# Last layer's attention: two heads' probabilities turned together, values stationary by pairs, output made turned

## The reference, cut to what matters

```python
def attention(x, kv_d_w, q_d_w, k_u_w, v_u_w, q_u_w, rope_k_w, rope_q_w, o_w):
    ...
    scores = jnp.einsum('bqhd,bkhd->bhqk', q, k) * scale
    causal = jnp.tril(jnp.ones((s, s), dtype=bool))
    scores = jnp.where(causal[None, None], scores, jnp.finfo(scores.dtype).min)
    probs = jax.nn.softmax(scores, axis=-1)
    out = jnp.einsum('bhqk,bkhd->bqhd', probs, v).reshape(b, s, H)
    return out @ o_w
...
h = x + attention(rmsnorm(x, ln1_w), kv_d_w, q_d_w, k_u_w, v_u_w, q_u_w, rope_k_w, rope_q_w, o_w)
out = h + moe(rmsnorm(h, ln2_w), sh_gate, sh_up, sh_down, r_gate, r_up, r_down, router_w, router_b)
```

## Time and profile before

| | us |
|---|---|
| median of three runs | 3743.81 (3738.99 to 3747.11) |
| profiled execution | 3749.25 |
| its span, first to last instruction | 3747.5 |
| PE busy | 3031.9 (81%) |
| DVE busy | 2278.8 (61%) |
| ACT busy | 1506.0 (40%) |
| POOL busy | 535.2 (14%) |

### The profile page before, as it was taken

How to read it: one execution, slowest core, us unless ns; L and a number is a source line. 1 busy time by engine, 2 the same in 40 slices (tenths; PEclk the granted TensorE clock), 3 DMA queues, 4 the chain that set the end, 5 groups by cost and what they waited for, 6 DMA issues and landing times. The chain is left out here.

```text
span 3747.5 us, 63586 instructions
## 1 busy us (share of the span) xinstructions
PE 3031.9 (81%) x23988; PEld 2108.2 (56%) x24036; DVE 2278.8 (61%) x4830; ACT 1506.0 (40%) x3074; POOL 535.2 (14%) x791
## 2 busy tenths in 40 slices
PE   7677789988776888857996868789898978787878
PEld 3333368867664556534664435355555556676767
DVE  6888844442558888865655732367777754444453
ACT  4777721111346455443442112155545532223332
POOL 3101000000002222111110022222212111111000
PEclk8766689988887776768998979899999988898787
DMA  4877740000010000010002040000000021000000
GB/s 125 164 159 164 160 135 0 0 22 0 14 56 2 2 2 2 2 69 9 6 12 69 0 135 22 3 4 3 3 6 3 3 87 51 1 0 0 1 1 12
DMA packets 316495, 141.38 MB, mean 38 GB/s; under 512 B 296221, under 2 KB 305953, under 8 KB 312613
## 3 DMA queue, kind: packets, MB, share of 16 engines
q1 hardware_dynamic: 308072, 138.45, 13.7%
q10 hardware_dynamic: 8256, 0.52, 0.2%
HBM read 67.65 MB, written 3.15 MB: 19 GB/s over the span
## 5 line engine op out<-in xcount | busy, mean ns | idle before, releaser
L1238 ACT ACTIVATE l0x_pb<-l0x_ex,l0x_neg_max,l0x_q_scale 128x2048 uint16<-128x2048 f32 x128 | 267.8, 2093 | 108.2 <-POOL l0x_neg_max L1319 106.5
L1139 PE MATMUL l0x_s_ps<-l0x_kT,l0x_qT 128*128 128x512 bf16 x466 | 206.5, 539 | 111.3 <-DVE l0x_ex L1416 51.8
L1413 DVE TENSOR_SCALAR_CACHE_REDUCE l0x_ex<-l0x_s_ps 128x1024 f32<-128x1024 f32 x128 | 156.4, 1222 | 46.1 <-PE l0x_s_ps L1139 35.0
L1416 DVE TENSOR_SCALAR_CACHE_REDUCE l0x_ex<-l0x_s_ps,l0x_first_max 128x1024 f32<-128x1024 f32 x128 | 164.3, 1284 | 16.7 <-DVE l0x_ex L1413 0.5
L1139 PEld LDWEIGHTS l0x_s_ps<-l0x_kT,l0x_qT 128*128 128x128 bf16 x512 | 39.2, 111 | 204.8 <-DVE l0x_ex L1416 140.5
L263 PE MATMUL l3x_bank<-l3x_w_kv_x,l3x_ctxT 128*128 128x512 f32 x256 | 120.1, 613 | 26.6 <-ACT l3x_ctx_k L762 15.8
L1147 PEld LDWEIGHTS l0x_o_ps<-l0x_v,l0x_vT 128*128 128x128 f16 x2048 | 78.6, 104 | 59.1 <-issue 41.8
L2198 PEld LDWEIGHTS l1a_bank<-l1a_u,l1a_gm 64*64 64x64 f32 x2048 | 95.5, 194 | 15.6 <-issue 14.8
L2190 PE MATMUL l1a_bank<-l1a_r,l1a_r 32*64 32x64 f32 x2048 | 75.9, 287 | 35.0 <-DVE l1a_r L2532 33.6
L263 PE MATMUL l2f_bank<-l2f_w,l2f_ln_yT 128*128 128x352 f32 x256 | 103.5, 539 | 0.0
L2198 PE MATMUL l1a_bank<-l1a_u,l1a_gm 64*64 64x8 f32 x2048 | 98.4, 235 | 4.7 <-DVE l1a_gm L2551 4.7
(11 more groups left out here) (747 smaller groups left out, 7838.0 us busy)
## 6 DMA issues: line engine op xcount, KB each, us to landing
l2f_wproj_raw<-in_L_xattn_wproj SPq DMA_DIRECT2D x2, 2048.0 KB, 12.3
l3a_w<-in_L_attn_W SPq DMA_DIRECT2D x4, 1024.0 KB, 11.3
l2f_w<-in_L_ffn_w SPq DMA_DIRECT2D x1, 2816.0 KB, 11.6
l0x_ex<-in_ctxT SPq DMA_DIRECT2D x8, 256.0 KB, 5.0
l0a_wq<-in_L_attn_W_Q SPq DMA_DIRECT2D x1, 2048.0 KB
l0a_wk<-in_L_attn_W_K SPq DMA_DIRECT2D x1, 2048.0 KB
l0x_vT<-l0x_pb SPq DMA_TRANSPOSE x128, 3.6
l0a_wv<-in_L_attn_W_V SPq DMA_DIRECT2D x1, 2048.0 KB, 7.8
```

Source lines behind the costliest of these rows:

```text
L1139: ins = mm(s_ps[:, j * 512:(j + 1) * 512], qT[:, h, :], kT[:, h // 2, j * 512:(j + 1) * 512], start=True, stop=True)
L1238: s.activation(pb[:, h % 4, :], ex[:, h % 4, :], ACT.Exp, scale=q_scale[:, h:h + 1], bias=nb[:, h:h + 1], accum_out=sums[:, h:h + 1]).then ...
L1413: v.tensor_scalar(ex[:, h % 4, 0:1024], s_ps[:, 0:1024], 1.0, None, ALU.mult, ALU.max, accum_out=first_max[:, h:h + 1]).then_inc(o.up(scor ...
L1416: v.tensor_scalar(ex[:, h % 4, 1024:2048], s_ps[:, 1024:2048], 1.0, first_max[:, h:h + 1], ALU.mult, ALU.max, accum_out=mx[:, h:h + 1]).th ...
```

## The change

In softmax `e` now stays as it is (queries in partitions, heads by keys along them), and no diagonal blocks are built. One transpose takes two neighbouring heads: 2 x 64 keys become the 128 partitions, the queries of both sequences the columns. The values lie to match: for each sequence and each pair of heads `vv` is 128 x 32, the even head's keys and its 16 elements in the upper left, the odd head's in the lower right, zeros elsewhere. It is stationary now, and 64 columns of `pt` (the queries of one sequence) move. Four pairs write to the four groups of 32 partitions of `first`, so the output comes out turned, element by query. The sums come from a product of their own with `same_head`, 128 x 32 with two blocks of ones, stationary, and 128 moving columns: every sum stands 16 times, once for each element of the head. DVE takes the reciprocal of these 128 x 256 values and multiplies into `outT`. The values product is cut into four, so that even heads land in the upper and odd heads in the lower 64 partitions. Gone are `pb`, `out`, the second round of turning, the turning of the output and its copy; each engine's program has two rounds fewer.

```diff
-    HV = HD + 1
+    PAIRS, TWO = H // 2, 2 * HD
...
+        same_head = L.sb("same_head", [P, TWO])
+        rows_of = tuple(slice(n * S, (n + 1) * S) for n in range(2))
...
-            qT, vv = L.sb("qT", [P, H, P]), L.sb("v", [P, H, HV])
+            qT, vv = L.sb("qT", [P, H, P]), L.sb("v", [P, 2, PAIRS, TWO])
             pt = qT
-            e, pb = L.sb("e", [P, H, S]), L.sb("pb", [P, H, P])
-            mx, inv = L.sb("mx", [P, H]), L.sb("inv", [P, H])
-            out, outT, h = L.sb("out", [P, H, HD]), L.sb("outT", [P, DC, P]), L.sb("h", [P, D])
+            e = L.sb("e", [P, H, S])
+            mx, inv = L.sb("mx", [P, H]), L.sb("inv", [P, D])
+            outT, h = L.sb("outT", [P, DC, P]), L.sb("h", [P, D])
...
                 def turn(n):
                     for i in range(4):
-                        ins = nc.tensor.transpose(bank[n % 2][:, i * P:(i + 1) * P], pb[:, 4 * n + i, :], env.ident[:])
+                        u = 8 * n + 2 * i
+                        ins = nc.tensor.transpose(bank[n][:, i * P:(i + 1) * P], e[:, u:u + 2, :].rearrange("p u k -> p (u k)"), env.ident[:])
                     ins.then_inc(pT_ps.sem, 1)
...
                 pe.wait_ge(qk_ready.sem, qk_ready.value(t, 1))
-                mm(first[:, 0:D], lat[:], v_lat[:], start=True, stop=True).then_inc(heads_ps.sem, 1)
+                pe.sem_inc(order["pe"], 1)
+                for b in range(2):
+                    for n, r in enumerate(rows_of):
+                        own_heads = v_lat[:].rearrange("p (i n d) -> p n i d", n=2, d=HD)[:, n, :, :]
+                        ins = mm(first[r, b * P:(b + 1) * P], lat[:, b * S:(b + 1) * S], own_heads, start=True, stop=True)
+                ins.then_inc(heads_ps.sem, 1)
                 yield
                 pe.wait_ge(qk_ready.sem, qk_ready.value(t))
-                pe.wait_ge(lat_v_ready.sem, lat_v_ready.value(t, 2))
+                pe.wait_ge(lat_v_ready.sem, lat_v_ready.value(t))
...
                 pe.wait_ge(exped.sem, exped.value(t))
-                for n in (0, 1):
+                for n in range(2):
                     turn(n)
                 yield
-                for n in (2, 3):
-                    pe.wait_ge(pT_ready.sem, pT_ready.value(t, n - 1))
-                    turn(n)
-                yield
-                for n in (3, 4):
-                    pe.wait_ge(pT_ready.sem, pT_ready.value(t, n))
-                for i in range(H):
-                    ins = mm(first[:, i * HV:(i + 1) * HV], pt[:, i, :], vv[:, i, :], start=True, stop=True)
-                ins.then_inc(out_ps.sem, 1)
-                yield
-                pe.wait_ge(out_ready.sem, out_ready.value(t))
+                pe.wait_ge(pT_ready.sem, pT_ready.value(t))
+                pe.sem_inc(order["pe"], 1)
                 for c in range(DC):
-                    ins = nc.tensor.transpose(other[:, c * P:(c + 1) * P], out[:, 8 * c:8 * c + 8, :].rearrange("p h d -> p (h d)"), env.ident[:])
+                    for b in range(2):
+                        for i in range(4):
+                            mm(first[32 * i:32 * i + 32, c * P + b * S:c * P + (b + 1) * S], vv[:, b, 4 * c + i, :], pt[:, 4 * c + i, b * S:(b + 1) * S], start=True, stop=True)
+                    for i in range(4):
+                        ins = mm(first[32 * i:32 * i + 32, D + c * P:D + (c + 1) * P], same_head[:], pt[:, 4 * c + i, :], start=True, stop=True)
                 ins.then_inc(out_ps.sem, 1)
...
-                    s.activation(flat(pt[:, 4 * n:4 * n + 4, :]), bank[n % 2][:], ACT.Copy).then_inc(o.up(pT_ready), 1)
+                    s.activation(flat(pt[:, 4 * n:4 * n + 4, :]), bank[n][:], ACT.Copy).then_inc(o.up(pT_ready), 1)
...
-                s.activation(vv[:, :, 0:HD], first[:, 0:D].rearrange("p (h d) -> p h d", d=HD), ACT.Copy).then_inc(o.up(lat_v_ready), 1)
+                for n, r in enumerate(rows_of):
+                    s.activation(vv[r, :, :, n * HD:(n + 1) * HD], first[r, 0:D].rearrange("p (b i d) -> p b i d", b=2, d=HD), ACT.Copy).then_inc(o.up(lat_v_ready), 1)
                 yield from steps(2)
                 act.wait_ge(shifted.sem, shifted.value(t))
-                for b in range(2):
-                    r = slice(b * S, (b + 1) * S)
-                    s.activation(pb[r, :, r], e[r], ACT.Exp).then_inc(o.up(exped if b else None), 1)
+                s.activation(flat(e[:]), flat(e[:]), ACT.Exp).then_inc(o.up(exped), 1)
                 yield
                 take_turned(0)
                 take_turned(1)
-                yield
-                take_turned(2)
-                take_turned(3)
                 yield from steps(2)
-                act.wait_ge(out_ps.sem, out_ps.value(t, TURNED))
-                s.activation(flat(outT[:]), other[:, 0:D], ACT.Copy).then_inc(o.up(outT_ready), 1)
-                yield
...
-                yield from steps(10)
+                yield from steps(8)
...
-                yield from steps(4)
+                yield from steps(3)
                 dve.wait_ge(out_ps.sem, out_ps.value(t, MIXED))
-                both = first[:, 0:H * HV].rearrange("p (h d) -> p h d", d=HV)
-                v.reciprocal(inv[:], both[:, :, HD]).then_inc(o.up(), 1)
+                v.reciprocal(inv[:], first[:, D:2 * D]).then_inc(o.up(), 1)
                 dve.wait_ge(o.sem, o.at())
-                v.tensor_tensor(out[:], both[:, :, 0:HD], inv[:].unsqueeze(2).broadcast_to([P, H, HD]), ALU.mult).then_inc(o.up(out_ready), 1)
-                yield from steps(2)
+                v.tensor_tensor(flat(outT[:]), first[:, 0:D], inv[:], ALU.mult).then_inc(o.up(outT_ready), 1)
+                yield
...
+            pe.wait_ge(block_set.sem, block_set.value())
...
             for tile in tiles:
-                nc.scalar.activation(tile["blocks"][:], env.ident[:].unsqueeze(1).broadcast_to([P, H, P]), ACT.Copy, scale=0.0).then_inc(cleared.sem, 1)
+                nc.scalar.activation(tile["values"][:].rearrange("p b i d -> p (b i d)"), env.ident[:].unsqueeze(1).broadcast_to([P, 4, P]), ACT.Copy, scale=0.0).then_inc(cleared.sem, 1)
...
+            nc.gpsimd.memset(same_head[:], 0.0).then_inc(block_set.sem, 1)
+            pool.wait_ge(block_set.sem, 1)
+            for n, r in enumerate(rows_of):
+                nc.gpsimd.memset(same_head[r, n * HD:(n + 1) * HD], 1.0).then_inc(block_set.sem, 1)
+            pool.wait_ge(block_set.sem, block_set.value())
...
-                v.memset(tile["ones"], 1.0).then_inc(set_up.sem, 1)
                 v.memset(tile["shared_weight"], 1.0 / 8.0).then_inc(set_up.sem, 1)
```

More of the change, by code:

```diff
@@ L4260, in one_of_four @@
             LATENT, QK, VALUES = 1, 2, 3
-            MIXED, TURNED, PROJECTED = 1, 2, 3
-            heads_ps, lat_v_ready, qk_ready = L.sig("heads_ps", 3), L.sig("lat_v_ready", 2), L.sig("qk_ready", 2)
-            scores_ps, shifted, exped, pT_ps, pT_ready = L.sig("scores_ps"), L.sig("shifted"), L.sig("exped"), L.sig("pT_ps", 4), L.sig("pT_ready", 4)
-            out_ps, out_ready, outT_ready, logits_ps, scored = L.sig("out_ps", 3), L.sig("out_ready"), L.sig("outT_ready"), L.sig("logits_ps"), L.sig("scored")
+            MIXED, PROJECTED = 1, 2
+            heads_ps, lat_v_ready, qk_ready = L.sig("heads_ps", 3), L.sig("lat_v_ready", 3), L.sig("qk_ready", 2)
+            scores_ps, shifted, exped, pT_ps, pT_ready = L.sig("scores_ps"), L.sig("shifted"), L.sig("exped"), L.sig("pT_ps", 2), L.sig("pT_ready", 2)
+            out_ps, outT_ready, logits_ps, scored = L.sig("out_ps", 2), L.sig("outT_ready"), L.sig("logits_ps"), L.sig("scored")
             hid_ps, silu, hid_ready, hidT_ps, hidT_ready = (L.sig(x, NE) for x in ("hid_ps", "silu", "hid_ready", "hidT_ps", "hidT_ready"))
@@ L4486, in one_of_four @@
             return {"tensor": tensor_program, "scalar": scalar_program, "gpsimd": gpsimd_program, "vector": vector_program,
-                    "blocks": pb, "ones": vv[:, :, HD:HV], "shared_weight": cw[:, 0:1]}
+                    "values": vv, "shared_weight": cw[:, 0:1]}
         tiles = [one_of_four(n, bank[2 * n:2 * n + 2]) for n in range(WAYS)]
-        set_up, cleared = L.sig("set_up", 2 * WAYS), L.sig("cleared", WAYS)
+        set_up, cleared = L.sig("set_up", WAYS), L.sig("cleared", WAYS)
+        block_set = L.sig("same_head_set", 3)
         block = L.block()
```

## The result

| | before | after |
|---|---|---|
| median, us (lowest to highest, runs) | 3742.96 (3738.99 to 3747.11, 4) | 3699.54 (3692.00 to 3704.11, 4) |
| ratio to before (95% interval) | | 0.9881 (0.9867 to 0.9895) |
| profiled execution, us | 3749.25 | 3692.00 |
| last layer, first statistics of the norm to the last sum, us | 313.27 | 270.28 |
| last exponential to the first `h`, pass 1 / pass 2, us | 34.99 / 34.95 | 13.10 / 13.41 |

What follows compares the result with a forecast made beforehand. PE was busiest, mixing slow through its 128-column weight loads; after the change DVE's division binds. 20.7 us a pass, 2 x 20.7 = 41.4 us off the 3743.81 us median gives 3702.4 us, range 3697 to 3708.

Steps and rivals of the forecast that it cites:

- Exponential and turning: Before mixing: one exponential for two, gaining 1.07 us on tile 3; PE turns from 3483.10 for 1.97 us.
- Mixing: Tile 0's products on PE: 1.89 us at 1.2 GHz plus 0.2 drain; 1.41 us a tile at 2.4 GHz.
- nothing here goes faster than 29: In mixing on PE: no matmul takes under 29 ns, giving 1.41 us a tile at 2.4 GHz.
- Division: DVE's reciprocal of 256 elements 1.77 us, with product and gaps 2.27 us a tile, 9.1 for four; sets the pace.
- Output: After division: PE projects tiles 0 to 2 as outputs come; DVE starts L4465 right after the last division, 3496.27.
- After it: Around L241: PE idles 5 us before, 13 us at the lower clock carried over; 0, with 1.5 us either way.
- Start and values product: Layer start and tile 3's values product: memsets hidden; values between 0.2 us gained and 0.2 lost; both taken as 0.
- pairs only: Rival in mixing, chance 0.18: four column groups overlap no more than two; 3714.4 us, or 3706.0 if the clock rises.
- one after another: Rival in mixing, chance 0.05: no overlap of column groups; 6.8 or 3.4 us a tile, 3739.4 or 3712.0 us.
- The cheap reciprocal: Rival in division, chance 0.06: DVE needs only 0.92 us a tile, mixing binds; 23.3 us a pass, 3697.2 us.
- the drain at each change of group: Rival in mixing, chance 0.03: each change of column group drains PE, 0.33 us each, 9.8 us a tile; 3763.2 us.

Runs made afterwards that it cites:

- the run with the copy: Changed kernel with a plain copy of the 128 x 256 sums in place of their reciprocal: median 3691.02 us, ratio 0.9867.
- the two orders: Changed kernel with mixing products ordered one column group after another, or two groups by turns: 3703.26 us (ratio 0.989) and 3698.04 us in one run.
- The run with straight output: Changed kernel with probabilities stationary (64 columns), 34 columns moving, output turned and copied afterwards: median 3703.18 us, ratio 0.9883.
- its padded form: Straight-output kernel with the moving side padded with zeros from 34 to 64 columns: median 3698.44 us, ratio 0.9873; in a later comparison 3694.78 us.

## Why the prediction held, step by step

The forecast was 3702.4 us, the median is 3699.54. It summed to 20.7 us a pass, measured were 21.9 and 21.5. The mechanism held: narrow weights make mixing short, and then the reciprocal sets the pace. Two terms were off in size, both to the dear side; in pass 1 mixing of tile 0 gave 0.5 us more than forecast, the divisions 0.6, and what is ahead of mixing 0.1. The forecast stands within 3 us of the median, less than the 12 us by which the runs of one kernel scatter, so such closeness is partly luck.

- Exponential and turning. PE was to turn 1.11 us after the exponential starts, for 1.97 us; it was 1.10, and 1.90 to the start of mixing. The sixteen banks of the earlier trace rows became eight, and mixing never waits for ACT's copies.
- Mixing, the first mis-sized term. The prediction gave 1.89 us to tile 0 and 0.2 to the drain; the first reciprocal came 1.60 us after mixing started in pass 1 and 1.90 in pass 2. At 1.2 GHz the rates were nearly right: in the rows below 16 matmuls with 64 moving columns take 0.43 us (27 ns each, 29 forecast) and the 8 with 128 take 0.43 us (54 each, 60 forecast). What the sum missed is that the clock rises within tile 0, which it had left at 1.2 GHz. Together 0.2 to 0.5 us a pass. At 2.4 GHz the step "nothing here goes faster than 29" failed: there the 64-column ones are 14 ns apart (0.22 us for 16, 3473.59 to 3473.81 above), and a tile takes 0.88 us, not 1.41. 29 ns in the earlier trace rows is what two halves by turns give, and was taken for a floor of the engine. This error cost the forecast nothing, only because the division hides the tiles behind the first.

```profile
3470.47 0.65 PE L4324 MATMUL l3f_bank<-l3f_qT,l3f_v 128*32 128x64 f32 x16
3470.90 0.65 PE L4326 MATMUL l3f_bank<-l3f_qT,l3f_same_head 128*32 128x128 f32 x8
3471.33 0.45 PE L4324 MATMUL l3f_bank<-l3f_qT,l3f_v 128*32 128x64 f32 x16
```

- Division, the second. The reciprocal was sized at 1.77 us from the earlier trace rows; all eight lie between 1.747 and 1.758 us:

```profile
L4455 DVE RECIPROCAL l3f_inv<-l3f_bank x8: 1747/1748/1758, 3472.1 to 3614.7; 128x256 f32<-128x256 f32 x8
```

The tile came to 2.12 us and not 2.27, for the product and the next reciprocal overlap:

```profile
3473.86 0.42 DVE L4457 TENSOR_TENSOR l3f_outT<-l3f_bank,l3f_inv 128x256 f32<-128x256 f32 x1
3474.21 1.75 DVE L4455 RECIPROCAL l3f_inv<-l3f_bank 128x256 f32<-128x256 f32 x1
```

The product starts at 3473.86 with 0.42 us, and the reciprocal starts 0.35 us later. The prediction had added a gap of 0.04 us to each; the one behind the reciprocal is there, the one behind the product isn't. Four tiles are 8.50 us in place of 9.1. That DVE sets the pace was the central claim, and the run with the copy confirms it.
- Output. The projection of tile 0 was to be done by the end of the last division; `h` starts at 3480.57, 0.34 us after the last product starts (3480.23), with no wait. Right.
- After it. PE idled 5.36 us before L241 (5 predicted) and L241 took its 1.97 us at the lower level. The granted clock rose at about 3498.7, 11.5 us after L241, where 13 had been carried over from the earlier trace rows; DVE's routing is the bound in that stretch, so the difference doesn't show. Worth 0, right: `h` to the first last sum is 64.53 us against 64.46, 64.28 against 64.27 in the second pass.

```profile
3487.20 1.97 PE L241 MATMUL l3f_bank<-ident,l3f_rms_y 128*128 128x128 f32 x8 [5.36 <-DVE l3f_rms_y L224]
```

- Start and values product. Up to the last exponential pass 1 has 0.29 us less than before, a little more than the 0.2 us of gain that was allowed: from the first values product of tile 3 to the first score it is 0.87 us in place of 1.15. POOL's memsets (0.12 and 0.27 us) aren't waited for.

Of the rivals, "pairs only" and "one after another" fell in the trace of the changed kernel and by the two orders; both had been priced too high (1.18 and 2.33 us a tile at 2.4 GHz, where 1.89 and 3.4 stood). The cheap reciprocal fell by 1.75 us, and the drain at each change of group by the 18.4 ns from one matmul to the next, with no "issue" but 0.33 us ahead of the first load. The chance given to "pairs only", 0.18, was a chance for 1.89 to 3.7 us a tile against 1.41 to 1.89; the orders measured 1.18 against 0.88.

What the prediction didn't see is how little of the gain hangs on the stationary values. It credited mixing's fall from 22.80 us to narrow weights, and rightly; but these don't need the values to be stationary. The run with straight output has 64-column weights and 128 matmuls, as many as before, and takes 7.05 us at 1.2 GHz for it, and its padded form 4.44 with the clock rising on the way. Pairing and 64-column weights carry the gain, and the turned output trades a turn and a copy for 1.5 us more of reciprocal a tile.

## What to carry to other kernels

Weights in disjoint groups of columns, issued by turns, overlap: the order of the loop decides (48.6, 24.6 and 18.4 ns a matmul for one, two and four groups), so put the group innermost. Before a denominator is replicated by a block of ones so that the output comes out turned, price the reciprocal by its elements a partition (0.26 us for 16, 0.96 for 128, 1.75 for 256, some 6.2 ns for each more): two small spreading products, or a turn of the output, were cheaper here. And ask of a stage not only how many matmuls it has but at which granted clock it runs; a stage that gains a higher clock is worth it only where PE is the bound next.

## What the runs showed of the hardware

- A stream padded with zeros ran faster than the unpadded one. 128 matmuls with 64 stationary columns took 7.05 us with 34 moving columns (granted clock 0.50 throughout) and 4.39 to 5.92 us in four passes with 64 (the clock rises on the way).
- Four groups of 32 columns by turns bring 14 ns from one matmul with 64 moving columns to the next at 2.4 GHz and 27 at 1.2 GHz, 27 and 54 with 128 moving columns, and 18.4 on average over a tile at 2.4 GHz. The Trainium skill, TensorE: Matmul & The Clock Gate, section "Wait — 56ns, not 53.3ns?", states of back-to-back matmuls that start-to-start never drops below about 25 ns; with groups by turns the measured averages of 14 and 18.4 ns are below that.
- A matmul of 32 stationary columns with nothing beside it costs 48.6 ns at 2.4 GHz, on average over a tile of 32 with 64 moving columns and 16 with 128; the four groups by turns gain 2.6 of the 4 that full overlap would give.
- In a dense stream of these narrow products, twice as long as the changed kernel's, PE stood still at two places for 0.70 and 1.31 us, and at the same places of the second pass for 0.26 and 1.04, with no cause in the profile. Open.
